# A four-layer decoder kernel: four-bit rounding by adding and removing a multiple of the exponent, its gate by tanh, and the last mixture's router and gate pieces at new places

## The reference, cut to what matters

```python
def fp4_quant_dequant(x):                      # blocks of 16 along the last dim
    scale = jnp.maximum(jnp.max(jnp.abs(xb), axis=-1, keepdims=True) / 6.0, 1e-12)
    xn = xb / scale
    idx = jnp.searchsorted(_MID, jnp.abs(xn))  # _MID .25 .75 1.25 1.75 2.5 3.5 5
    return _GRID[idx] * jnp.sign(xn) * scale   # _GRID 0 .5 1 1.5 2 3 4 6
gate, y = fp4_linear(x, w_gate), fp4_linear(x, w_up)   # both operands rounded; 352 wide
h = jax.nn.silu(gate) * y
return fp4_linear(h, w_down)                           # h rounded too
```

## Time and profile before

| | us |
|---|---|
| median of 3 runs | 1363.23 |
| lowest, highest | 1358.95, 1364.07 |
| the profiled execution | 1366.51 |
| its span in the trace | 1365.2 |

### The profile page before, as it was taken

The page is one execution under the profiler, slowest core; times in us unless marked ns, Lnnn a source line. Parts: engine busy times, 40 slices in busy tenths (PEclk is TensorE's granted clock), DMA queues, the critical chain, the costliest instruction groups (busy, mean ns, idle before and its releaser), DMA issues.

```text
span 1365.2 us, 18663 instructions
## 1 busy us (share of the span) xinstructions
PE 1049.8 (77%) x7025; PEld 557.7 (41%) x7025; DVE 844.0 (62%) x2052; ACT 610.7 (45%) x1001; POOL 232.5 (17%) x299
## 2 busy tenths in 40 slices
PE   3475769998999964767767899897477667568999
PEld 2132213333577642434432335465122223235757
DVE  5674767741215468888767844866888676564422
ACT  1143425664334437766725784231045454433332
POOL 2452310000000133765420000001000000010000
PEclk8576759999899985767777998998668687778999
DMA  4663140000000310441024004001003000000000
GB/s 125 187 230 122 38 173 2 2 2 1 0 1 1 89 36 0 140 137 51 1 99 161 2 2 109 21 0 47 1 24 117 1 2 1 31 0 1 1 8 8
DMA packets 47682, 67.43 MB, mean 49 GB/s; under 512 B 4904, under 2 KB 41977, under 8 KB 45897
## 3 DMA queue, kind: packets, MB, share of 16 engines
q1 hardware_dynamic: 46872, 65.19, 14.9%
q10 hardware_dynamic: 720, 1.05, 0.3%
HBM read 46.83 MB, written 19.01 MB: 48 GB/s over the span
## 4 chain that ended last, share of the span: by engine, by line
PE 51%; DVE 30%; issue 5%; DMA 5%; ACT 4%; POOL 2%; SPq 2%; DVEq 0%; ACTq 0%; POOLq 0%
PE ps_e L739 8%; PE ps_s L749 8%; PE ps_v L581 6%; DVE mx L1678 5%; PE ps_e L527 5%; PE ps_s L546 3%; PE ps_e L525 3%; DVE work L2056 3%; DVE ps_s L1674 2%; DMA q_scr<-parts 2%; DVE work L2156 2%; ACT work L1233 2%; PE ps_e L833 2%; PE ps_s L820 2%; DVE work L2158 2%
## 5 line engine op out<-in xcount | busy, mean ns | idle before, releaser
L1233 ACT ACTIVATE work<-ps_e 128x512 f32<-128x512 f32 x448 | 250.7, 597 | 170.0 <-PE ps_e L527 164.3
L527 PE MATMUL ps_e<-q_stack,ctx_stack 52*128 52x256 bf16 x768 | 153.6, 303 | 31.0 <-ACT work L1233 23.2
L1678 DVE TENSOR_REDUCE mx<-ps_s 128x2 f32<-128x1024 f32 x128 | 154.1, 1222 | 37.0 <-PE ps_s L546 35.5
L2429 POOL TENSOR_TENSOR rstd<-rstd,halves 128x2 f32<-128x2 f32 x52 | 36.6, 704 | 814.4 <-DVE rstd L1621 814.2
L546 PE MATMUL ps_s<-ctx_stack,q_stack 49*128 49x512 bf16 x384 | 133.4, 470 | 45.2 <-DVE mx L1678 30.5
L1326 ACT ACTIVATE work<-ps_s,keep 128x512 f32<-128x512 f32 x136 | 93.1, 687 | 145.9 <-PE ps_s L749 142.8
L581 PE MATMUL ps_v<-work,vaug 128*32 128x256 f32 x1536 | 137.6, 437 | 8.1 <-ACT work L1221 8.1
L739 PEld LDWEIGHTS ps_e<-ffn_w,work 128*128 128x128 f32 x960 | 120.7, 200 | 23.6 <-issue 19.4
L749 PE MATMUL ps_s<-xnT,ffn_w 128*128 128x512 f32 x240 | 119.8, 628 | 7.6 <-ACT work L1326 7.6
L739 PE MATMUL ps_e<-ffn_w,work 128*128 128x128 f32 x960 | 123.1, 284 | 2.6 <-DVE x L1869 2.4
L1674 DVE CUSTOM_DVE_ANT_0 ps_s<-ps_s,work 128x512 f32<-128x512 f32 x128 | 85.9, 716 | 47.3 <-PE ps_s L546 47.2
(11 more groups left out here) (361 smaller groups left out, 1823.2 us busy)
## 6 DMA issues: line engine op xcount, KB each, us to landing
q_stack<-q_scr SPq DMA_DIRECT2D x40, 192.0 KB
ctx_stack<-c_scr SPq DMA_DIRECT2D x4, 1536.0 KB
ffn_w<-in_L0f_w SPq DMA_DIRECT2D x1, 4608.0 KB, 15.5
q_scr<-parts SPq DMA_DIRECT2D x20, 192.0 KB, 2.1
ffn_w<-in_L1f_w SPq DMA_DIRECT2D x1, 3456.0 KB, 14.1
self_stack<-k_scr SPq DMA_DIRECT2D x16, 192.0 KB
ctx_stack<-kx_scr SPq DMA_DIRECT2D x2, 1536.0 KB
ffn_w<-in_L3f_w SPq DMA_DIRECT2D x1, 3072.0 KB, 13.0
```

What stands on the lines that cost most here:

```text
L527: m = pe.matmul(bank[name][:, half * S:(half + 1) * S], stack[p0:p0 + K_EXP, pair, b * nk + k * P:b * nk + (k + 1) * P], q_stack[p0:p0 + K ...
L1233: act.activation(pt[:, parity, :, :].rearrange("p k q -> p (k q)"), bank[f"e{parity}"], ACT.Exp).then_inc(exped, 1)
L1678: m = dve.tensor_reduce(mx[:, b, :, pair, part], ps_s[i][:], AX, ALU.max, negate=True)
```

## The change

The rounding (`f4_steps`) no longer compares with seven thresholds. It scales by the block's scale (times the number just below one, in one instruction), takes the exponent by masking the bits, turns it into 3 x 2^21 times the power of two, adds that and subtracts it again, so that the addition rounds to the grid. Sign and magnitude are not taken apart, and ACT has no part in it. The gate is `(tanh(g/2) + 1) * g`, then `* 0.5 * up`: Tanh on ACT in place of Silu, two instructions a tile on DVE in place of one. The steps of the chain move: x is rounded at 4 and 5, transposed at 7, gate and up at 9, the hidden values rounded at 10 to 12 and transposed at 15; what follows stands one slot later, up to step 35, and step 36 stays. In the tail `route_rest` comes a slot later, "bias" is split into "gate" and "bias", both go ahead of the third unit's up pieces, and the pieces are spread anew over the slots.

```diff
-PIECES = [("up", u, k) for u in range(3) for k in range(2)] + [("bias", 0, 0)]
+PIECES = [("up", u, k) for u in range(3) for k in range(2)] + [("gate", 0, 0), ("bias", 0, 0)]
+PIECES[4:8] = PIECES[6:8] + PIECES[4:6]
...
-PIECES_BEFORE = {96: 3, 98: 1, 100: 4, 101: 3, 102: 3, 104: 1, 107: 2, 109: 1, 111: 1, 114: 2, 116: 1, 118: 1, 120: 1, 124: 5}
+PIECES_BEFORE = {95: 2, 96: 1, 97: 1, 98: 1, 99: 2, 101: 1, 102: 1, 103: 1, 104: 1, 105: 1, 106: 1, 107: 1, 108: 1, 109: 1,
+                 110: 1, 111: 1, 113: 1, 114: 2, 116: 1, 117: 1, 118: 1, 120: 1, 122: 2, 123: 2, 124: 1}
...
@@ ACT @@
-        def f4_halves(kind, n):
-            a, mag, sgn, sc, rs = f4_work(kind)
-            act.wait_ge(f4_in, n + 1)
-            act.activation(sgn, mag, ACT.Sign, scale=0.5)
-            act.activation(mag, mag, ACT.Abs).then_inc(f4_parts, 1)
...
-                            act.activation(hbuf[:, i * F2:(i + 1) * F2], ps_s[s][:, 0, 0:F2], ACT.Silu).then_inc(silu_done, 1)
+                            act.activation(hbuf[:, i * F2:(i + 1) * F2], ps_s[s][:, 0, 0:F2], ACT.Tanh,
+                                           scale=0.5).then_inc(silu_done, 1)
...
@@ DVE, l3_tail @@
             route_first("L3f", 0, half[0])
-            chain(TAIL0)
-            route_rest("L3f", 1e-8, 0, half[0])
             n = 0
-            for t in range(TAIL0 + 1, LAST["chain"]):
+            for t in range(TAIL0, LAST["chain"]):
+                if t == TAIL0 + 1:
+                    route_rest("L3f", 1e-8, 0, half[0])
...
@@ DVE, the rounding: i is the step, v and big 128-partition fp32 buffers @@
-                settle(dve.tensor_scalar(a, mag, 5.0, 2.0, ALU.is_gt, ALU.mult))
-            elif i == 3:
-                settle(dve.tensor_scalar(a, a, 2.0, None, ALU.mult))
-            elif i < 8:
-                mid = (3.5, 2.5, None, 1.75, 1.25, 0.75, 0.25)[i - 1]
-                settle(dve.scalar_tensor_tensor(a, mag, mid, a, ALU.is_gt, ALU.add))
-            elif i == 8:
-                settle(dve.scalar_tensor_tensor(a, a, 0.5, sgn, ALU.mult, ALU.mult))
-            else:
-                dve.tensor_tensor(blk(src), blk(a), wide(sc), ALU.mult).then_inc(done, 1)
+                elif i == 3:
+                    settle(dve.scalar_tensor_tensor(blk(v), blk(src), BELOW_ONE, wide(rs), ALU.mult, ALU.mult))
+                elif i == 4:
+                    settle(dve.tensor_scalar(big.bitcast(I32), v.bitcast(I32), EXPONENT_BITS, None, ALU.bitwise_and))
+                elif i == 5:
+                    settle(dve.tensor_scalar(big, big, 1.0, HALF_STEPS, ALU.max, ALU.mult))
+                elif i == 6:
+                    settle(dve.tensor_tensor(v, v, big, ALU.add))
+                elif i == 7:
+                    settle(dve.tensor_tensor(v, v, big, ALU.subtract))
+                else:
+                    dve.tensor_tensor(blk(src), blk(v), wide(sc), ALU.mult).then_inc(done, 1)
...
@@ DVE, chain @@
                 if at == 4:
                     dve.wait_ge(norm_out, NORM_AT["L2f", b])
-                    f4_first(kT[:, cols(b)], "x")
-                if at == 6:
-                    for i in range(10):
-                        f4_step(kT[:, cols(b)], "x", i, 2 * b + 1, f4_x)
-                if at == 10:
+                    f4_steps(kT[:, cols(b)], "x", range(5), f4_x)
+                if at == 5:
+                    f4_steps(kT[:, cols(b)], "x", range(5, 9), f4_x)
+                if at == 9:
...
-                        dve.tensor_tensor(h, h, ps_s[s][:, 1, 0:F2], ALU.mult).then_inc(hidden, 1)
+                        settle(dve.scalar_tensor_tensor(h, h, 1.0, ps_s[s][:, 0, 0:F2], ALU.add, ALU.mult))
+                        dve.scalar_tensor_tensor(h, h, 0.5, ps_s[s][:, 1, 0:F2], ALU.mult, ALU.mult).then_inc(hidden, 1)
+                if at == 10:
                     dve.wait_ge(hidden, F2_HID0 + 2 * b + 2)
-                    f4_first(hbuf, "h")
+                    f4_steps(hbuf, "h", range(4), f4_x)
+                if at == 11:
+                    f4_steps(hbuf, "h", range(4, 7), f4_x)
                 if at == 12:
-                    for i in range(4):
-                        f4_step(hbuf, "h", i, 2 * b + 2, f4_x)
-                if at == 13:
-                    for i in range(4, 10):
-                        f4_step(hbuf, "h", i, 2 * b + 2, f4_x)
+                    f4_steps(hbuf, "h", range(7, 9), f4_x)
```

More of the change, by code:

```diff
@@ L61 @@
 FP4_BLOCK = 16
+EXPONENT_BITS = 0x7F800000
+HALF_STEPS = float(3 << 21)
+BELOW_ONE = 1.0 - 2.0 ** -23
 VA = H * (D + 1)
@@ L127, in order_of @@
     return {p: i + 1 for i, p in enumerate(pairs)}
-CHAIN = [("L2f", 3), ("L3a", 16), ("L3x", 23), ("L3x-inner", 32), ("L3f", 33)]
+CHAIN = [("L2f", 3), ("L3a", 17), ("L3x", 24), ("L3x-inner", 33), ("L3f", 34)]
 tail = sorted((close_slot(X2, b) + at, b, st) for st, at in CHAIN for b in range(B))
@@ L136 @@
 NORM_AT = order_of(front + [p for p in tail if p[0] != "L3x-inner"])
-TURNS = [("L2f", 8), ("L3a", 19), ("L3x", 26), ("L3f", 36)]
+TURNS = [("L2f", 7), ("L3a", 20), ("L3x", 27), ("L3f", 36)]
 turned_tail = sorted((close_slot(X2, b) + at, b, st) for st, at in TURNS for b in range(B))
@@ L425, in f4_work @@
         sc_at = 2816 if kind != "w" else at + 3 * n
-        return [wk(at + i * n, n) for i in range(3)] + [wk(sc_at, nb), wk(sc_at + nb, nb)]
+        return [wk(at + i * n, n) for i in range(2)] + [wk(sc_at, nb), wk(sc_at + nb, nb)]
     def chain_steps(slot):
@@ L711, in route, with turn_gates @@
             free[name] = (route_in, ROUTE_AT[st] + g)
-        def gated_bias(st, which, n, g, routed):
+        def turn_gates(st, n, g, routed):
             pe.wait_ge(gated, routed)
-            count = BIAS0[st] + g + 1
             claim("e1")
@@ L719, in gated_bias @@
             m.then_inc(gate_ps, 1)
-            free["e1"] = (gate_T, count)
+            free["e1"] = (gate_T, BIAS0[st] + g + 1)
+        def gated_bias(st, which, n, g):
+            count = BIAS0[st] + g + 1
             claim("e0")
@@ L789, in l3_piece @@
                     gelu_up("L3f", g * NE + e, j)
+            elif kind == "gate":
+                turn_gates("L3f", NE, g, ROUTE_AT["L3f"] + g)
             elif kind == "bias":
-                gated_bias("L3f", 1, NE, g, ROUTE_AT["L3f"] + g)
+                gated_bias("L3f", 1, NE, g)
             else:
@@ L1866, in gated_bias @@
             dve.tensor_copy(gatesT[0:n, g * 512:(g + 1) * 512], ps_e[1][0:n, :]).then_inc(gate_T, 1)
+        def gated_bias(st, g):
+            count = BIAS0[st] + g + 1
             dve.wait_ge(bias_ps, count)
@@ L1890, in l0_mixture @@
             for g in range(2):
-                gated_bias("L0f", n_exp, g)
+                turn_gates("L0f", n_exp, g)
+                gated_bias("L0f", g)
             for u in range(2 * n_exp):
@@ L1906, in l3_piece @@
             kind, e, k = PIECES[i]
-            if kind == "bias":
-                gated_bias("L3f", NE, g)
+            if kind == "gate":
+                turn_gates("L3f", NE, g)
+            elif kind == "bias":
+                gated_bias("L3f", g)
             elif kind == "down":
@@ L1992, in swiglu_window @@
             if v == 5:
-                f4_first(f2_raw, "w")
-            if 8 <= v < 18:
-                f4_step(f2_raw, "w", v - 8, 0, f4_w)
+                dve.wait_ge(d_w2, 16)
+                f4_steps(f2_raw, "w", range(3), f4_w)
+            if 8 <= v < 14:
+                f4_steps(f2_raw, "w", range(v - 5, v - 4), f4_w)
             if v in (19, 21, 23):
@@ L2033, in wide @@
             def wide(t):
-                return t.unsqueeze(2).broadcast_to([P, nb, FP4_BLOCK])
-            return a, mag, sgn, sc, rs, blk, wide
-        def f4_first(src, kind):
-            a, mag, sgn, sc, rs, blk, wide = f4_views(kind)
-            if kind == "w":
-                dve.wait_ge(d_w2, 16)
-            settle(dve.tensor_reduce(sc, blk(src), AX, ALU.max, apply_absolute_value=True))
-            settle(dve.tensor_scalar(sc, sc, 1.0 / 6.0, 1e-12, ALU.mult, ALU.max))
-            settle(dve.reciprocal(rs, sc))
-            dve.tensor_tensor(blk(mag), blk(src), wide(rs), ALU.mult).then_inc(f4_in, 1)
@@ new lines, in f4_steps @@
+            for i in steps:
+                if i == 0:
+                    settle(dve.tensor_reduce(sc, blk(src), AX, ALU.max, apply_absolute_value=True))
+                elif i == 1:
+                    settle(dve.tensor_scalar(sc, sc, 1.0 / 6.0, 1e-12, ALU.mult, ALU.max))
+                elif i == 2:
+                    settle(dve.reciprocal(rs, sc))
+                elif i == 3:
[10 more added lines that the diff above has]
+                    dve.tensor_tensor(blk(src), blk(v), wide(sc), ALU.mult).then_inc(done, 1)
```

94 lines of the change are left out of this document (42 added, 52 removed).

## The result

The changed kernel takes 1299.28 us, median of 4 runs (1296.19 to 1304.24), beside 1361.09 us of the kernel before; the ratio is 0.9556 [0.9505, 0.9607]. Measured a second time, the same kernel gave 1304.49 us (6 runs), ratio 0.9592 [0.9556, 0.9629]; the median of all ten runs is 1302.8 us. So by the medians the change is worth 58 to 62 us, where 53 were forecast. The profiled execution took 1301.29 us, span 1300.0.

A forecast was written before the change was run, and what follows sets the result against it. The prediction took hand-overs around L2f's rounding as the bound, no engine full. Terms 12 + 22 + 3 + 12 + 3 + 1 = 53 us gave 1310 from the median; own range 1298 to 1324 (48%), 8 in 10 range 1288 to 1339.

The forecast's parts named there:

- What bounds the kernel: Around L2f's rounding no engine is full; PE waits on hand-overs, 18.2 us around batch 0, 28.7 around batches 1 and 2.
- only the instructions count: Rival, 20%: PE's waits are replaced by others, leaving only DVE's and ACT's own gain, 1337 us.
- the moved slots: Batch 0: hidden-value transposes, moved from 14 to 15, get two slots of slack behind the rounding, 1.5 us more.
- the second half: Second half of L3f: the bias addition is covered by two up pieces, gain 1 us.
- Instructions: Roundings and gate: DVE saves 4.5 us per 128x704 rounding, 2.1 per 128x256; the gate costs 1.0 more a batch.
- Table loads: ACT at Silu and Tanh: all eight loads go; four on PE's path make 5.1 us between the two ends.
- Batch 0: Slots 44 to 56, where DVE will be the bound: gain 12 of the 18.2 us of waits.
- Batches 1 and 2: Behind slot 63 DVE has room without maxima: three quarters of 28.7 us of waits go, gain 22 us.
- the clock term: PE from 1092 to 1207: granted clock from 0.73 to 0.85 saves 11 us of matmuls; a quarter counted, 3 us.
- The tail: Last mixture: waits for Gelu, turned gates, bias and norm go, and a low clock ends; gain 12 us.
- Weights: Rounding at 850 to 890: five DVE instructions go and PE's wait of 2.1 us ends; gain 3 us.
- What would have shown it wrong: PE waits above 3 us ahead of other steps, DVE holding batches 1 and 2, or a tail piece awaiting `route_rest`.

The follow-up runs named there:

- the rounding alone: The kernel before with the new rounding everywhere and no ACT passes, keeping old slots, Silu and old tail: 1299.28 us, ratio 0.9544.
- the second trace: A second profiled execution of the changed kernel, not a line different: 1301.41 us; batches 1 and 2 took 80.9 us at clock 0.83.
- the best version: The kernel before with the new rounding and the new tail, keeping old slots and Silu: 1294.53 us, ratio 0.9508.

## Why the prediction was right, point by point

*What bounds the kernel* held: hand-overs around the rounding, no engine full. Both halves of the rounding, its round trip to ACT and its length on DVE, are real. Each alone, put back, costs 17 to 21 us (round trip) and 38 to 42 us (DVE's passes); together that is at least the 55 us that the rounding of x and h gave (1354.5 to 1299.3). The rival "only the instructions count" falls by the round trip's run, and its 1337 us by the result. What is right in it is that DVE's passes count, and here for more than their own length, 38 for 26.5.

*Luck in the sum*: that the forecast of 53 us was only 5 to 9 us short is partly two errors that cancel. The forecast gave about 7 us to the moved slots (1.5 in batch 0), to the places in the tail (4.3) and to the second half (1); taken together, the moved slots, Tanh and the new places bring nothing over the rounding alone (1299.28 us for it, 1299.28 and 1304.49 for the changed kernel). The rounding, priced at about 46 us, is worth 62.

*Instructions*: right at each size (mask 0.521 us, the tensor_tensor 0.89, gate 0.52).

*Table loads*: none at Tanh, right in the trace. The Trainium skill ("ScalarE: Activation LUTs", Table sets) has tanh in the set of exp; the trace agrees, with no load at any of the 8. Their price was wrong in kind. The forecast gave Tanh a worth between 0 and 5.1 us, always positive. It is 3 to 4 us in the kernel before, 6 us in the new slots and minus 6 us in the old slots with the new rounding. Tanh takes one more DVE instruction of 0.52 us per tile, 4.2 us in all; that DVE's time in front of the transposes costs more than its length would explain the loss, but no run shows it for this instruction.

*Batch 0*: forecast 12 us, measured 10.6; PE's wait for the exponentials there, 8.4 us, is gone, and what is left is the maxima, 6.2 us:

```profile
PE ps_s L550 <- DVE mx L1676: 6.2, 5, 2.5
PE ps_s L501 <- DVE mx L1676: 2.3, 1, 2.3
```

*Batches 1 and 2 and the clock*: forecast 22 and 3 us. The waits gave 17.7 to 18.5 (the forecast took the 6.9 us at L581 for a wait for exponentials; it shrank to 2.6 all the same), and the clock term was the mis-sized one: PE's busy time fell by 10.1 to 16.4 us, where a quarter of 11 was counted. The reason given for the quarter, that faster matmuls aren't always what the next step waits for, is right for batch 0. After the change PE's own work comes through in this stretch: of 6.2 us more of it in the second trace, 5.4 reach the stretch's end. I should have asked of the kernel after, not of the one before, which engine sets the pace.

*The tail and the second half*: forecast 12 and 1 us, measured 11.5 (9.9 in the second trace) from batch 3's first statistics on. Its sign came true: from the first piece to the last norm statistics the tail took 69.1 us, 78.8 before, where about 70 was forecast, and no piece waits for `route_rest`. The split was 7.6 for the end of the rounding and of its activations and 4.3 for the places. The rounding alone gave 11.3 us in these stretches with the old places, and the new places 6.1 on top, so both were too small; Tanh and the new slots took 6 back. Of the waits named, that for Gelu went from 4.7 to 0.7 us and the 2.9 us for the norm behind batch 3's rounding of x is gone; that for the turned gates grew from 0.9 to 1.9, where it was to go:

```profile
PE ps_m L478 <- DVE xn L1632: 6.2, 2, 5.4
PE ps_e L731 <- DVE parts L1864: 1.9, 1, 1.9
...
PE ps_s L755 <- ACT work L1335: 0.7, 1, 0.7
```

The 5.4 us at L478 in these rows isn't the wait that was named. It stands at batch 3's own L2f norm, right behind the cut, and the kernel before has it just ahead of the cut, with 3.5 us:

```profile
PE ps_m L474 <- DVE xn L1634: 4.0, 2, 3.5
```

It is 3.5 us in the traces of all kernels with the old slots, whatever their rounding, and 4.7 to 5.4 us in those of all kernels with the new ones. So it belongs to the moved slots.

*Weights*: forecast 3 us, measured 7.5 aligned and 7 by median. Of 7.5 us, 2.8 are PE's busy time (53.1 to 50.3, at 0.97 and 1.00) and 4.7 its waits; I had counted one wait of 2.1 us and 1 us beside it, and of the clock nothing.

*What would have shown it wrong*: a wait above 3 us ahead of another chain step is there, the 5.4 us of L478 at the border of the tail, of which 3.5 were there before, and the transposes' wait was 1.8 us, not below 1. Both together are a few us of 60.

## What to carry to other kernels

Where a stage has hand-overs and no full engine, a shorter computation on the engine in the middle is worth more than its length, and an activation that waits for another engine costs what is queued behind it. Add one part of a change at a time: here the moved slots cost time, Tanh gained some of it back but costs time in the old slots once the rounding is short, and the best version leaves both out. Ask of a clock gain which engine is the bound once the change is in, and profile the same kernel twice before giving a few us of one stretch a cause.

## What the runs showed of the hardware

TensorE's granted clock in one stretch of an unchanged program was 0.95 in one execution and 0.83 in another, worth 5.4 us there and 9.3 us over the last third, while the whole differed by 0.1 us: in the second trace the part ahead of the first cut was 9.4 us shorter. The Trainium skill ("TensorE: Matmul & The Clock Gate", What's actually happening) says that the count of slow matmuls at the start of a kernel differs from run to run. These two traces show such a difference too, but in the middle of the kernel, where the 9.3 us are 2% of the last third's 458. A bitwise_and on int32 took DVE 0.521 us for 704 elements a partition, like the fp32 tensor_scalar (0.527) and unlike the two-tensor forms (0.89). Filling an idle TensorE with 22 matmuls of 512 columns (0.379 us each) lifted the granted clock of 109 us only from 0.73 to 0.76.
